# Self-attention: VectorE copies the second pair's 16-bit probabilities from the 32-bit ones, and its own low part stands one maximum sooner

## The reference

```python
qn = _rmsnorm(q, q_gamma) * dh ** (-0.5)
kn = _rmsnorm(k, k_gamma)
sim = jnp.einsum('bhid,bhjd->bhij', qn, kn)
attn = jax.nn.softmax(sim, axis=-1)
out = jnp.einsum('bhij,bhjd->bhid', attn, v)
```

## Time and profile before

| | us |
|---|---|
| median of 3 runs | 2322.66 |
| lowest and highest | 2322.13, 2323.05 |
| the profiled execution | 2315.09 |
| its span, first to last instruction | 2313.3 |
| TensorE busy in the span | 2178.3 |
| ScalarE, VectorE, GpSimd busy | 1612.0, 1552.2, 1542.5 |

### The profile page before, as it was taken

The page is one execution under the profiler, slowest core; times in us unless marked ns, Lnnn a source line. Parts: engine busy times, 40 slices in busy tenths (PEclk is TensorE's granted clock), DMA queues, the critical chain, the costliest instruction groups (busy, mean ns, idle before and its releaser), DMA issues. The chain is left out here.

```text
span 2313.3 us, 62611 instructions
## 1 busy us (share of the span) xinstructions
PE 2178.3 (94%) x22392; PEld 1254.6 (54%) x22392; DVE 1552.2 (67%) x2573; ACT 1612.0 (70%) x1831; POOL 1542.5 (67%) x1008
## 2 busy tenths in 40 slices
PE   6988999999997989899989899999999978998999
PEld 3544666666665455444445456666666644554444
DVE  5897777777776666753368977777777767667532
ACT  3556999999998556731145579999999975566210
POOL 5644988989988577721246368998989976867210
PEclk9999999999999999999999999999999999999999
DMA  4220000000001301103112100000000022021000
GB/s 105 56 49 3 4 7 9 9 9 9 9 0 28 100 6 39 46 12 81 46 51 56 42 1 10 0 9 9 9 9 9 9 61 64 2 47 38 19 23 33
DMA packets 102348, 65.23 MB, mean 28 GB/s; under 512 B 75346, under 2 KB 75346, under 8 KB 102226
## 3 DMA queue, kind: packets, MB, share of 16 engines
q1 hardware_dynamic: 102226, 63.57, 12.5%
HBM read 46.69 MB, written 8.39 MB: 24 GB/s over the span
## 5 line engine op out<-in xcount | busy, mean ns | idle before, releaser
L597 POOL TENSOR_TENSOR qkn<-wide 128x1024 f16<-128x1024 f32 x448 | 986.7, 2234 | 136.5 <-PE bank L710 120.7
L909 DVE TENSOR_REDUCE sq<-bank 128x1 f32<-128x512 f32 x1024 | 679.8, 688 | 246.8 <-PE bank L666 244.1
L836 ACT ACTIVATE wide<-bank,shift 128x1024 f32<-128x1024 f32 x512 | 571.0, 1115 | 37.3 <-DVE qkn L923 30.7
L828 ACT ACTIVATE wide<-bank,shift 128x1024 f16<-128x1024 f32 x512 | 568.1, 1110 | 9.9 <-PE bank L682 9.9
L681 PE MATMUL bank<-q_hh,ko 128*128 (+1 forms) x1024 | 388.9, 380 | 18.5 <-ACT wide L836 13.6
L666 PE MATMUL bank<-ko,q_hh 128*128 (+1 forms) x1024 | 387.7, 380 | 10.7 <-DVE sq L909 7.1
L682 PE MATMUL bank<-q_lm,k_h 65*128 (+1 forms) x1024 | 389.0, 380 | 0.0
L695 PEld LDWEIGHTS bank<-v_hl,wide 128*128 128x128 f16 x4096 | 287.6, 98 | 63.4 <-issue 5.7
L695 PE MATMUL bank<-v_hl,wide 128*128 (+1 forms) x4096 | 320.0, 192 | 0.1
L697 PE MATMUL bank<-v_hl,wide 128*128 (+1 forms) x4096 | 318.1, 193 | 0.0
L697 PEld LDWEIGHTS bank<-v_hl,wide 128*128 128x128 f16 x4096 | 267.5, 96 | 58.7
(11 more groups left out here) (228 smaller groups left out, 4213.2 us busy)
## 6 DMA issues: line engine op xcount, KB each, us to landing
wide<-in_x SPq DMA_DIRECT2D x32, 256.0 KB, 2.7
q_lm<-in_x SPq DMA_DIRECT2D x32, 256.0 KB, 3.2
ko<-in_L_ffn_W SPq DMA_DIRECT2D x32, 256.0 KB, 4.1
q_hh<-q_hh SPq DMA_DIRECT2D x32, 128.0 KB, 2.6
ko<-k_h SPq DMA_DIRECT2D x32, 128.0 KB, 2.8
out<-bo_b SPq DMA_DIRECT2D x16, 256.0 KB, 2.0
out<-xbo_b SPq DMA_DIRECT2D x16, 256.0 KB, 2.0
q_lm<-sq SPq DMA_DIRECT2D x248, 0.2 KB, 4.9
```

The costliest lines, as they stand in the source:

```text
L597: pool.tensor_tensor(probs_l[:, p % 2, :], probs[:, p % 2, :], probs_h[:, p % 4, :], ALU.subtract).then_inc(pl_pool, 1)
L828: act.activation(probs_h[:, p % 4, :], SB[p % 2][:, :], ACT.Exp, bias=shift[:, 0:1]).then_inc(ph_ready, 1)
L836: act.activation(probs[:, p % 2, :], SB[p % 2][:, :], ACT.Exp, bias=shift[:, 0:1]).then_inc(p_ready, 1)
L909: dve.tensor_reduce(pm[:, s, k:k + 1], MB[k % 2], AX_X, ALU.max).then_inc(mx_free, 1)
```

## The change

ScalarE no longer runs H(1). Instead VectorE makes the 16-bit probabilities of pair 1 from the 32-bit ones, as the maximum of a tile with itself written as 16-bit. Here it is called C. It needs F(1) and signals a new semaphore, `ph_dve`. The values matmuls of the high part of pair 1 and GpSimd's L(1) wait for that semaphore. In VectorE's order C stands behind R(1) (behind R(7) of the unit ahead in the first unit), and L(4) stands behind R(9) instead of R(10). `ph_ready` counts 7 a unit instead of 8.

```diff
@@ gpsimd, low parts
                                 pool.wait_ge(p_ready, G + p + 1)
+                                if p == CAST:
+
+                                    pool.wait_ge(ph_dve, U0 + u + 1)
+                                    pool.nop(nofuse=True)
 
                                 pool.wait_ge(lo_done, G + p + 1)
@@ tensor, values_high
-                            pe.wait_ge(ph_ready, (U0 + u) * PAIRS + p + 1)
+                            if p == CAST:
+                                pe.wait_ge(ph_dve, U0 + u + 1)
+                            else:
+                                pe.wait_ge(ph_ready, (U0 + u) * (PAIRS - 1) + (p if p < CAST else p - 1) + 1)
@@ scalar, exponentials
-                                act.activation(probs_h[:, p % 4, :], SB[p % 2][:, :], ACT.Exp, bias=shift[:, 0:1]).then_inc(ph_ready, 1)
+                                if p != CAST:
+                                    act.activation(probs_h[:, p % 4, :], SB[p % 2][:, :], ACT.Exp, bias=shift[:, 0:1])\
+                                        .then_inc(ph_ready, 1)
@@ vector
+                        def probs_high(u):
+                            p = CAST
+                            dve.wait_ge(p_ready, (U0 + u) * PAIRS + p + 1)
+                            dve.tensor_tensor(probs_h[:, p % 4, :], probs[:, p % 2, :], probs[:, p % 2, :], ALU.max)\
+                                .then_inc(ph_dve, 1)
+
...
                                 if maxed:
                                     reduce_max(u + LA, k, s)
+                                if k == 1 and not first:
+                                    probs_high(u)
                                 if k == 4 and not first:
                                     output(u - 1, 1 - s)
-                                if k == (6 if first else 2 * (DVE_PAIR + 1)):
+                                if k == (6 if first else 2 * DVE_PAIR + 1):
                                     probs_low(u)
```

More of the change, by code:

```diff
@@ L227, in decoder_layer @@
         ph_ready = sem("ph_ready")
+        ph_dve = sem("ph_dve")
         p_ready = sem("p_ready")
@@ L496, in decoder_layer @@
                     AHEAD = 6
+                    CAST = 1
                     vf = v_hl
@@ L953, in unit @@
                                     reduce_max(1, k, 1)
+                                    if k == 7:
+                                        probs_high(u)
                                 negate_max(1, 1)
```

## The result

| | before | after |
|---|---|---|
| median, us | 2322.39 | 2379.16 |
| lowest and highest | 2320.96, 2323.05 | 2376.78, 2381.07 |
| span of the profiled execution | 2313.3 | 2375.0 |

The change makes the kernel slower by 2.45%: the ratio is 1.0245, with a 95% interval from 1.0227 to 1.0263. The forecast was 2380.3 us.

The account below looks back on a forecast made before the run. GpSimd's low parts and, ending last, TensorE's slots up to V(3) were taken to bound a 17.10 us unit. +0.9 us for 30 units plus 1.8, over two batches, adds 57.6 to 2322.66: 2380.3 us, 8-in-10 range 2352 to 2406.

Parts of the forecast that it names:

- part 1: ScalarE without H(1): takes away 1.0 us a unit, but F(1) waits for L(7), so worth nothing at F(1).
- walk: Step-by-step timing of one self-attention loop unit, from L(5)'s start to the next L(5): 17.95 us.
- part 2: C on VectorE reads SBUF twice, waits for GpSimd's L(0) and ends 1.10 us after it, at 9.49.
- R(2), M(4), TensorE: R(2) stands behind C, so M(4) starts at 10.15; TensorE stalls about 1.4 us; next L(5) at 17.95.
- the hiccup of every second unit: About 0.3 us in TensorE's slot 0, mostly covered by its new stall; 0.05 us added a unit.
- part 3: L(4) one maximum sooner runs in GpSimd's idle time; GpSimd's 0.63 and ScalarE's 0.46 us a unit given back.
- The sum: +0.9 us for 30 units and 1.8 for the last two: 28.8 a batch, 57.6 for both.
- The signs: Expected in the profile after: C near 2.0 us, M(4) waiting about 1.4, ScalarE's loop busy share near 90%.
- The free copy: Rival: C's two inputs are one tile and share memory freely; +0.1 us a unit, 2329 us; chance 0.10.
- The faster case: Rival: F(1) starts when H(1)'s time is free, only L(4)'s move counts; -0.5 us a unit, 2293; chance 0.05.
- The case in which the delay grows: Rival: R(9) later, L(4) meets L(5), or low parts 5 to 7 wait; 18.6 us a unit, 2417; chance 0.07.

Follow-up runs that it names:

- no_high1: Kernel before without H(1) and without C, pair 1's values matmul and L(1) reading pair 0's tile instead: 2319.6 us, ratio 0.9997.
- copy_alone: Changed kernel with L(4) back behind R(10), so the copy C without the L(4) move: 2414.74 us, ratio 1.0404.
- low_sooner_alone: Kernel before with only L(4) moved to behind R(9), H(1) kept on ScalarE, no C: 2293.11 us, ratio 0.9882.

## Why the prediction was right

**F(1) is held by L(7), part 1.** Right, and shown by no_high1. In the unit above L(7) ends 6.31 us after L(5)'s start (walk: 6.30), F(1) starts 0.04 later.

**C waits for L(0), part 2.** Right. It ends at 9.56 in that unit (walk: 9.49), 1.08 us behind L(0)'s end; the estimate from L(4)'s one blocked row was 1.10. That the same tile twice counts as two reads was a choice without a row; C's 1995 ns in the changed kernel, against 1216 where nothing held it, bear it out. The Trainium skill's rule (SBUF — State Buffer, "Who interferes with whom") is that two SBUF inputs on VectorE contend with a GpSimd instruction that reads SBUF. This trace agrees: C took 2.0 us with two inputs, and 1.22 as the reduction with one.

**R(2), M(4), TensorE.** Right. M(4) starts at 10.30 (walk: 10.15), V(3) ends at 17.95 (17.80), the next L(5) starts at 18.10 (17.95). I had added 0.05 for the hiccup of every second unit; the mean is 18.05. The stall itself is 1.23 us of idle time a unit in the wait table; 1.4 was M(4)'s lateness.

**L(4) in GpSimd's gap, part 3.** Right. It runs from 16.32 on (16.25) and meets no low part. I said that the walk would be about 0.6 longer without that move; copy_alone says 0.58. For the kernel before, though, I had put GpSimd's 0.63 us beside ScalarE's 0.46 as what the move gives back. GpSimd's part is not on the chain there: the 0.47 us of low_sooner_alone come from M(13) and slot 7, which waited for what L(4) held on VectorE and ScalarE.

**The sum** came out right in part by luck. Its terms were a little small. The 28 steps from the L(5) of unit 1 to that of unit 29 grew by 0.93 us each, not 0.9. Unit 1 costs 1.3 us more, not 0.9. The last two were right: from L(5) to L(5) they take 17.15 instead of 16.51 us (+0.64; I had +0.6) and 19.87 instead of 18.61 (+1.26; +1.2). That makes 30.2 us in either batch instead of 28.8. Another 1.3 us of the span lie outside self-attention, and no run shows why. So the span grew by 61.7 us and not by 57.6, yet the medians differ by 56.8 us only. The profiled execution of before was a quick one, 7.6 us under the median of its runs, and I carried that distance over; the changed kernel's (2376.78) is only 2.4 under. The two errors, 4.1 us too little and 5.2 too much, cancel to the 1.1 us between forecast and result.

**The signs.** One was off: ScalarE's busy share in the loop fell to 87% (424.26 of 487.25 us), where I had said near 90%. My own figures give 87 too: 449.42 us less 27 exponentials of 1.04, over 27 units of 18.0.

**The rivals.** The free copy would have given 2329 by the walk, and the run that makes it true gave 2326.77. The faster case named 2293 for part 3 alone, and that run gave 2293.11. Its premise, that ScalarE's time is worth something at F(1), is what failed it. The case in which the delay grows did not come about.

## What to carry to other kernels

An engine that is 97% busy can still be following another: look whether its instructions start a fixed few hundredths of a microsecond behind the end of someone else's (F(1) 0.04 us behind L(7)), and if so, taking work from it gives only idle time. Before moving work to a less busy engine, ask what stands behind it in that engine's order, and whom that holds (here one reduction and one matmul turned a copy into 1.2 us of stall on TensorE). When VectorE works beside GpSimd, ask of each operation whether it waits there, and look for another form: the copy with one tile as both inputs waited, the same copy written as a reduction over an axis of one is as fast and didn't. The number of inputs alone doesn't tell, as the scalar operation with one input that took 2.62 us instead of 0.68 shows.

## What the hardware showed that I had not expected

- A stall on TensorE can cost more than its length. With 1.23 us of stall a unit the granted clock stayed at 1.00 through the loop, and the same with waits near 1.5 us in copy_alone. Where stalls of 1.8 to 1.9 us came in every second unit it was 0.98 over 400 us, falling in some of these units; with 2.3 us and more in each unit it was 0.92, falling in every unit, and M(4) took 0.61 us instead of 0.38. One fall cost 1.2 to 1.4 us of a unit.
- A VectorE reduction over an axis of one element works as a copy from 32 to 16 bits: 1.22 us for 128 x 1024, the same as the operation with two inputs (1.22 us where nothing held it), and beside GpSimd's low parts it varied by 2 ns.
